# First attention with one pass of scores and transposed exponentials, and a new order at the second attention's start

## What is computed

```python
attn = jnp.einsum('bhqd,bhkd->bhqk', q, k) * SCALE      # first attention
mask = jnp.triu(jnp.full((s, s), -jnp.inf), k=1)
attn = softmax(attn + mask, axis=-1)
out = jnp.einsum('bhqk,bhkd->bhqd', attn, v)
...
logits = xf @ router_w.T                                 # experts
top_vals, top_idx = jax.lax.top_k(logits, 2)
out = out + combine[:, e:e + 1] * y                      # y: expert e's gated MLP
...
x = x + attn_a(layernorm(x)); x = x + ffn(layernorm(x))
x = x + attn_b(layernorm(x)); x = x + ffn(layernorm(x))
```

## Time and profile before

| | |
|---|---|
| median of three runs | 893.17 us (891.84 to 893.41) |
| the profiled execution | 890.42 us, its span 888.8 us |
| PE busy over the span | 778.6 us (88%) |
| DVE, ACT, POOL busy | 355.7, 285.2, 249.7 us |
| the chain that ended last | PE 80%, DVE 7%, DMA 5% |

### The profile page before, as it was taken

How to read it: one execution, slowest core, us unless ns; L and a number is a source line. 1 busy time by engine, 2 the same in 40 slices (tenths; PEclk the granted TensorE clock), 3 DMA queues, 4 the chain that set the end, 5 groups by cost and what they waited for, 6 DMA issues and landing times.

```text
span 888.8 us, 14689 instructions
## 1 busy us (share of the span) xinstructions
PE 778.6 (88%) x4924; PEld 592.6 (67%) x4925; DVE 355.7 (40%) x902; ACT 285.2 (32%) x527; POOL 249.7 (28%) x322
## 2 busy tenths in 40 slices
PE   5999999999989999999936389988879999999990
PEld 3777777787757677777725257666656767777760
DVE  4452553544434222222246477676463422212211
ACT  2103114031423334334222124534534234343321
POOL 1541043143034222212133313253641411211213
PEclk9999999999999999999977689999998999999995
DMA  7389933036971143002030722220401101110004
GB/s 191 68 259 329 318 100 92 10 78 234 340 199 49 40 164 117 34 25 77 18 107 18 216 50 52 51 65 7 163 29 39 66 31 35 35 35 24 30 19 148
DMA packets 48124, 88.10 MB, mean 99 GB/s; under 512 B 8913, under 2 KB 37329, under 8 KB 45937
## 3 DMA queue, kind: packets, MB, share of 16 engines
q1 hardware_dynamic: 36743, 54.56, 21.8%
q0 software_dynamic: 7568, 30.97, 9.5%
q10 hardware_dynamic: 3760, 1.87, 0.7%
HBM read 52.04 MB, written 35.03 MB: 98 GB/s over the span
## 4 chain that ended last, share of the span: by engine, by line
PE 80%; DVE 7%; DMA 5%; issue 2%; ACT 2%; POOL 2%; SPq 1%; ACTq 0%; POOLq 0%; DVEq 0%
PE bank L1423 24%; PE bank L1450 13%; PE bank L912 10%; PE bank L465 4%; PE bank L513 4%; PE bank L1436 4%; PE bank L525 2%; PE bank L455 2%; PE bank L546 2%; PE bank L511 2%; PE bank L589 2%; DVE XN L609 2%; PE bank L563 1%; DMA q_parts<-XN 1%; PE bank L1410 1%
## 5 line engine op out<-in xcount | busy, mean ns | idle before, releaser
L1423 PE MATMUL bank<-wgu,R 128*128 x736 | 224.8, 458 | 0.8 <-ACT R L1458 0.7
L1423 PEld LDWEIGHTS bank<-wgu,R 128*128 128x128 f32 x736 | 137.6, 192 | 66.0 <-issue 3.8
L1450 PE MATMUL bank<-R 112*128 (+1 forms) x552 | 127.0, 379 | 1.2 <-ACT R L1472 1.2
L1450 PEld LDWEIGHTS bank<-R 112*128 112x128 f32 (+1 forms) x552 | 104.4, 190 | 22.3 <-issue 1.7
L1488 DVE TENSOR_TENSOR R<-R,bank 128x344 f32<-128x344 f32 x92 | 47.2, 513 | 175.6 <-PE bank L1423 165.4
L658 ACT ACTIVATE PTR<-bank 128x512 f32<-128x512 f32 x144 | 78.8, 598 | 96.3 <-PE bank L513 83.2
L1399 POOL DMA_INDIRECT rows_out<-R,XN x46 | 45.4, 988 | 168.1 <-ACT R L1480 156.5
L1495 DVE COPY R<-bank 112x512 f32<-112x512 f32 x46 | 31.8, 690 | 103.8 <-PE bank L1436 103.8
L609 DVE TENSOR_REDUCE XN<-bank 128x2 f32<-128x512 f32 x96 | 63.2, 685 | 9.1 <-PE bank L465 9.1
L1466 ACT ACTIVATE R<-bank 128x344 f32<-128x344 f32 x92 | 41.9, 458 | 76.9 <-PE bank L1423 76.7
L829 POOL TENSOR_SCALAR_AFFINE_SELECT PTR<-PTR 128x512 f32<-128x512 f32 x64 | 39.7, 645 | 91.7 <-ACT PTR L658 91.6
(11 more groups left out here) (169 smaller groups left out, 1195.5 us busy)
## 6 DMA issues: line engine op xcount, KB each, us to landing
wgu<-in_wgu SPq DMA_DIRECT2D x10, 1376.0 KB, 15.5
slots_in<-wgu POOLq DMA_DIRECT2D x1, 9088.0 KB, 27.5
row_of_slot<-in_unused POOLq DMA_DIRECT2D x2, 4544.0 KB, 17.7
R<-slots_in SPq DMA_DIRECT2D x46, 128.0 KB, 2.0
wgu<-R SPq DMA_DIRECT2D x32, 128.0 KB, 2.4
R<-R SPq DMA_DIRECT2D x32, 128.0 KB, 2.4
R<-in_wd SPq DMA_DIRECT2D x8, 448.0 KB, 6.8
PTR<-rows_out SPq DMA_DIRECT2D x12, 256.0 KB, 4.5
```

Of the source, the lines that this page charges most:

```text
L1423: last = nc.tensor.matmul(BK[2 * half + gu][:, 0:IH], xsT[:, p, kk, :], wgu[:, bass.ds(e * (KD * GU) + (kk * GU + gu * I + half * IH), IH) ...
L1450: last = nc.tensor.matmul(down_bank(i)[:, 0:D], hT[0:CH[c], p, c, :], wd[0:CH[c], bass.ds(e * (6 * D) + c * D, D)], start=c == 0, stop=c == 5)
```

## The change

In the first attention the second pass, the split of the maxima and its transposes are gone. The scores of a group go to `bank0` to `bank2`; DVE takes the maxima and multiplies them by the scale (`maxima_a_vector`); ACT takes the exponentials with the maximum as a bias for each partition, in eight instructions for a group in place of three (`exps_a_scalar`), into a buffer in SBUF that exists once (`rows_of`: a part of expert 2's place, and `wob`). PE transposes the buffer in twelve pieces into `bank3` to `bank5` (`turned_tensor`), and ACT (two banks) and DVE (one) copy them to `PTR` (`moved_scalar`, `moved_vector`). One loop with n = 0 to 17 goes over the 16 groups of all batches: in step n PE does the scores of group n, the transposes of n-1, the turned output of n-3 and the value product of n-2. The finished batch b is projected at n = 4b + 7, normalised and routed at 4b + 8 and 4b + 9. Both projections for the first two batches stand ahead of the loop; the third's and fourth's are behind n = 3 and n = 7, and the next scores wait until they are evacuated. Expert 2 and `wob` are loaded later.

In the second attention the last part of q has a place of its own (`last_parts`, in `PTR`), so its split does not wait for an earlier store; DVE's wait for the stores moves from ahead of `parts_vector` to n = 1, and ACT gets one ahead of its first exponential; SP's order is shown below.

On PE, in the middle of the first batch, the second pass over one group of four heads stood like this before: one mask per bank, then for each head a product with the shift and the score product again (bank3 to bank5; the rows of bank4 and bank5 go on in the same way), and the value products into bank6.

The diff, cut to its core:

```diff
+        vaug3 = room(2 * KD * GU + 1024, 2 * HA * 32)
+        values_a = [vaug, vaug3, vaug2, vaug]
+
+        def rows_of(b):
+            o = 4 * HA * S // 2
+            two = room(2 * KD * GU, 1024) if b < B - 1 else R1[:, o:o + 1024]
+            return [two[:, 0:512], two[:, 512:1024], wob[:, :, :].rearrange("p k n -> p (k n)")]
...
-                elif i == 0 and g >= 2:
-                    nc.tensor.wait_ge(s["maxima"], b * 3 * G + 3 * (g - 1))
-                elif i == 0 and b > 0:
-                    nc.tensor.wait_ge(s["exps"], (b - 1) * 3 * G + 3 * (G - 1 + g))
+                else:
+                    later(nc.tensor, s["exps"], max(3 * (b * G + g - 1) + i + 1, 0))
...
-        def attend_a_tensor(b):
-            max_tensor(0, b)
-            nc.tensor.wait_ge(AT[0]["max_e"], b + 1)
-            for g in range(GA):
-                if g < 2 and b < B - 1:
-                    items = [i for i in BY_V if i < ITEMS - 3 or g == 1]
-                    nc.tensor.wait_ge(PA["evac_v"], (b + 1) * len(BY_V) + len(items))
...
+        RUN_A = B * GA
+
+        def turned_tensor(b, g):
+
+            s = AT[0]
+            n = b * GA + g
+            src = rows_of(b)
+            nc.tensor.wait_ge(s["exps"], 3 * n + 3)
+            if g == GA - 1 and b + 2 < B:
+                nc.tensor.wait_ge(PA["evac_v"], (b + 3) * len(BY_V))
+                nc.tensor.wait_ge(PA["evac_s"], (b + 3) * len(BY_S))
+            for i in range(2):
+                later(nc.tensor, s["moved_s"], max(2 * (n - 1) + i + 1, 0))
+                for j in range(2):
+                    c = 2 * i + j
+                    nc.tensor.transpose(BK[3 + i][:, j * S:j * S + P], src[0][:, c * P:(c + 1) * P], ident[:, :])
+                    last = nc.tensor.transpose(BK[3 + i][:, j * S + P:(j + 1) * S], src[1 + i][:, j * S:j * S + P], ident[:, :])
+                last.then_inc(s["turned"], 1)
+            later(nc.tensor, s["moved_v"], n)
+            for j in range(4):
+                o = (j % 2) * S + P
+                last = nc.tensor.transpose(BK[5][:, j * P:(j + 1) * P], src[1 + j // 2][:, o:o + P], ident[:, :])
+            last.then_inc(s["turned"], 1)
...
+        def attend_a_tensor():
+            for n in range(RUN_A + 2):
+                if n < RUN_A:
+                    scores_tensor(0, *of(n))
+                b = batch_at(n, 7)
+                if b is not None:
+                    project_tensor(0, b)
+                b = batch_at(n, 8)
+                if b is not None:
+                    norm_tensor(1, b)
+                ranked = batch_at(n, 9)
+                if ranked is not None and n < RUN_A:
+                    rank_tensor(1, ranked)
+                if 1 <= n <= RUN_A:
+                    turned_tensor(*of(n - 1))
+                if n >= 3:
+                    b = batch_at(n, 8)
+                    if b is not None:
+                        nc.tensor.wait_ge(LN[1]["evac"], b + 1)
+                    if ranked is not None and n < RUN_A:
+                        nc.tensor.wait_ge(FF[1]["slot"], ranked + 1)
+                    if ranked is not None and n >= RUN_A:
+                        nc.tensor.wait_ge(FF[1]["copied"], ranked + 1)
+                    out_t_tensor(0, *of(n - 3))
+                if n >= 2:
+                    pv_tensor(0, *of(n - 2))
+                b = batch_at(n, 6)
+                if b is not None:
+                    all_t_tensor(0, b)
+                b = batch_at(n, 8)
+                if b is not None:
+                    nc.tensor.wait_ge(AT[0]["divided"], n - 2)
+                    logits_tensor(1, b)
+                if ranked is not None and n >= RUN_A:
+                    nc.tensor.wait_ge(AT[0]["divided"], n - 2)
+                    rank_tensor(1, ranked)
+                if n < RUN_A and n % GA == GA - 1 and n // GA + 2 < B:
+                    project_a_tensor(n // GA + 2)
+            nc.tensor.wait_ge(FF[1]["slot"], B - 1)
...
+        def maxima_a_vector(b, g):
+            s = AT[0]
+            n = b * GA + g
+            bank = BK[0:3]
+            for i in range(3):
+                nc.vector.wait_ge(s["scores"], 3 * n + i + 1)
+                q, h, m = (0, 4 * g, 4) if i == 0 else (1, 4 * g + 2 * (i - 1), 2)
+                link(nc.vector.tensor_reduce(nrem[:, q, h:h + m], bank[i][:, :].rearrange("p (n s) -> p n s", n=m),
+                                             AX, ALU.max, negate=True))
+                nc.vector.tensor_scalar(nmax[:, q, h:h + m], nrem[:, q, h:h + m], SCALE_A, None,
+                                        ALU.mult).then_inc(s["maxima"], 1)
+
...
+        def moved_scalar(n):
+            s = AT[0]
+            for i in range(2):
+                nc.scalar.wait_ge(s["turned"], 3 * n + i + 1)
+                if i == 0:
+                    later(nc.scalar, s["pv"], max(n - 1, 0))
+                nc.scalar.activation(PT[:, n % 2, i, :], BK[3 + i][:, :], ACT.Copy).then_inc(s["moved_s"], 1)
...
+        def exps_a_scalar(b, g):
+            s = AT[0]
+            n = b * GA + g
+            dst = rows_of(b)
+            if g == 0 and b == B - 1:
+                nc.scalar.wait_ge(PA["placed_k"], B * PLACED_K)
+            for i in range(3):
+                nc.scalar.wait_ge(s["maxima"], 3 * n + i + 1)
+                if i == 0:
+                    later(nc.scalar, s["turned"], 3 * n)
+                q, h, m, w = (0, 4 * g, 4, P) if i == 0 else (1, 4 * g + 2 * (i - 1), 2, S)
+                for j in range(m):
+                    last = nc.scalar.activation(dst[i][:, j * w:(j + 1) * w], BK[i][:, j * w:(j + 1) * w], ACT.Exp,
+                                                bias=nmax[:, q, h + j:h + j + 1], scale=SCALE_A)
+                last.then_inc(s["exps"], 1)
...
+        def attend_a_vector():
+            for n in range(RUN_A + 2):
+                b = batch_at(n, 8)
+                if b is not None:
+                    normed_vector(1, b)
+                if n < RUN_A:
+                    maxima_a_vector(*of(n))
+                b = batch_at(n, 7)
+                if b is not None:
+                    add_vector(0, b)
+                    stats_vector(1, b, (AT[0]["added"], b + 1))
+                ranked = batch_at(n, 9)
+                if ranked is not None and n < RUN_A:
+                    slots_vector(1, ranked)
+                if 1 <= n <= RUN_A:
+                    moved_vector(n - 1)
+                if n >= 3:
+                    divide_vector(0, *of(n - 3))
+                if n >= 2:
+                    pv_vector(0, *of(n - 2))
+                b = batch_at(n, 8)
+                if b is not None:
+                    logits_vector(1, b)
+                    largest_vector(1, b)
+                if ranked is not None and n >= RUN_A:
+                    slots_vector(1, ranked)
+                if n < RUN_A and n % GA == GA - 1 and n // GA + 2 < B:
+                    project_a_vector(n // GA + 2)
+            full_tiles_vector(1)
...
+        def attend_a_scalar():
+            for n in range(RUN_A + 2):
+                b = batch_at(n, 8)
+                if b is not None:
+                    evac_scalar(1, b)
+                if n < RUN_A:
+                    exps_a_scalar(*of(n))
+                if 1 <= n <= RUN_A:
+                    moved_scalar(n - 1)
+                b = batch_at(n, 6)
+                if b is not None:
+                    out_scalar(0, b)
+                b = batch_at(n, 7)
+                if b is not None:
+                    root_scalar(1, b)
+                if n < RUN_A and n % GA == GA - 1 and n // GA + 2 < B:
+                    project_a_scalar(n // GA + 2)
...
-            nc.vector.wait_ge(PB["stored0"], 16 * 3)
-            nc.vector.wait_ge(PB["stored1"], 16 * (PARTS + 1))
             parts_vector(2, 0)
...
+                if n == 1:
+                    nc.vector.wait_ge(PB["stored0"], 16 * 3)
+                    nc.vector.wait_ge(PB["stored1"], 16 * (PARTS + 1))
                 if n >= 1:
                     pv_vector(2, (n - 1) // GB, (n - 1) % GB)
...
         def attend_b_scalar():
             max_scalar(2, 0)
+            nc.scalar.wait_ge(PB["stored0"], 16 * 3)
             for n in range(RUN):
...
             def store(i):
                 nc.scalar.wait_ge(s["lo"], i + 1)
+                if i == B:
+                    nc.scalar.wait_ge(s["stored0"], 16 * 2)
...
-                    elif i >= 2:
-                        nc.scalar.wait_ge(s["stored0"], 8 * i)
+                    elif i == 2:
+                        nc.scalar.wait_ge(s["stored0"], 16)
...
-            if b == 0:
-                nc.sync.wait_ge(PB["lo"], 2)
-                rows = k_r[0].rearrange("(j n i) h s -> n (i h) j s", j=2 * PARTS, n=PARTS)
-                for n in range(PARTS):
-                    nc.sync.dma_start(rows[n], qparts[0:32, 1, :, :]).then_inc(PB["stored1"], 16)
...
             if b == 0:
                 q_rows(0)
-                q_rows(1)
```

(15 more changed lines are left out.)

169 lines of the change are left out of this document (47 added, 122 removed).

## The result

The changed kernel takes 863.59 us (median of four runs, 859.38 to 872.76) against 892.5 for the kernel before, run beside it (890.19 to 893.41): a ratio of 0.9666, interval 0.9624 to 0.9707. With the six runs of the first experiment there are ten, from 859.0 to 872.8, with a median of 866.8; that is some 0.972 of the median before in the same two sets of runs (891.5). The kernel before, run beside every experiment, stayed between 888.7 and 897.0.

What follows compares the result with a forecast made beforehand. PE was taken to bound the first attention, DVE the second attention's start; 890.42 us less 17 (first expert tile earlier) and 7 (second attention) gave 866.4, and 2.75 up to the runs' median about 869; range 857 to 880.

Steps and rivals of the forecast that it cites:

- the likeliest case: Whole kernel: the median lies at 862 to 875 us, with 869 in it; chance 0.60.
- The step of the loop: First attention: one group's step takes 6.1 us, PE idling some 0.7; ends 5.9 and 6.8.
- The circle of one buffer: First attention: scores, transposes, overlap, four exponentials and hand-overs follow one another because the buffer exists once; 6.1 us.
- The twelve transposes: First attention, each step on PE: twelve transposes take 1.32 us, from four taking 0.44.
- the estimate of 901: First attention: at the skill's 275 ns, twelve transposes take 3.3 us, a step 8.1, the time some 32 more.
- I charge no clock for the loop: First attention's loop: PE's waits of 0.7 in 6.1 us leave the granted clock at 1.00; no cost.
- The rival of the falling clock: First attention's loop: at 1.2 GHz a step is 10.5 us, not 6.1; all sixteen give about 940; chance 0.05.
- The new wait for the root: First attention, n = 11: ACT's late square root delays PE's normalised rows by 2 us (0 to 4).
- The weights: Experts: weights are there by 213 us, needed at 238; a cover of 25 us, later loads cost nothing.
- The 7: Second attention's start: DVE's first maximum comes at about 501, not 507.75; worth 7 us (5 to 8).
- No wait bites: First attention: step 5.43 us, nothing lost to root or clock; gain 24 + 15, about 854; chance 0.12.
- DVE slowed by sharing PSUM: First attention's loop: DVE's work becomes 7.5 us a step, not 4.5; time about 891; chance 0.03.

Runs made afterwards that it cites:

- the first experiment: The changed kernel run once more with no edit, six runs: 868.25 us, ratio 0.9686.
- two_buffers: The changed kernel with a second buffer of exponentials for every other group, in expert 1's place, which is loaded last: 854.84 us, ratio 0.9591.
- tail_order: The changed kernel with the third batch's root, logits and rank put ahead at the end of the first attention: 860.1 us, ratio 0.9655.
- tail2_warm: tail_order with DVE's tile list right behind the slots and idle transposes ahead of first scores, third batch's normalising and first expert tile: 860.75 us, ratio 0.9657.
- gap0: The changed kernel with sixteen idle transposes in PE's wait ahead of the first scores: 863.93 us, ratio 0.9682.
- gap0_again: gap0 run once more, unchanged, for the count of runs: 860.08 us, ratio 0.966.
- the fill: The sixteen idle transposes ahead of the first scores, added to the changed kernel: 863.93 us in gap0, 860.08 us in gap0_again.
- second_part: The kernel before with only the second attention's edits: 883.63 us, ratio 0.9911.
- second_sp_old: second_part with SP's order as in the kernel before, both halves of q ahead of k's rows: 885.21 us, ratio 0.9934.

## Why the prediction was right, and where it was not

The time, 869 forecast, lies in the ten runs, and the likeliest case, 862 to 875, came in. The mechanism of the loop was right; that the number fits so well is in part luck, as the sum shows. Its steps:

- **The step of the loop.** Forecast 6.1 with 0.7 of waiting; measured 5.85 with 0.29 in a plain step. ACT's exponentials of 128 columns took 368 ns, 390 was taken. The circle of one buffer was the right mechanism: two_buffers breaks it.
- **The twelve transposes.** 1.32 forecast; from 206.94 to 208.26 twelve and the next product's start are 1.32 apart. The figure of 275 ns in the Trainium skill ("TensorE: Matmul & The Clock Gate", "Part 4: PE-mode transpose") agrees with how long one of this kernel's f32 transposes lasts, 0.27. But transposes overlap and start 0.11 apart, and the clock stands at 1.00 there. So the estimate of 901, which takes twelve such durations one behind the other, and the comparison by which the row "speaks for two fifths of that duration" mix a duration with the distance between starts.
- **"I charge no clock for the loop"** is the step that failed. The rival of the falling clock came in for two stretches, not for the loop: 9 us in the profiled execution. Its price was fair: the second step costs 4.0 more at the lower clock, and 4.4 was taken. The waits of 0.3 to 0.7 that I weighed are harmless (1.00 from 75 to 160); the first fall stands right behind the wait of 1.77 ahead of the first scores, which I had priced as time and not as an occasion. The second, from about 167, begins 9 us behind a wait of 1.38; what sets it off was not tried. The new wait for the root, priced at 2 as time, is an occasion too, in three other profiles.
- **The sum.** I had the last step ending at 210.4, so a start of 204.3 for group 15. Where the clock holds through the loop (tail_order, tail2_warm) it starts at 200.2 and 199.8, with one later fall (gap0, gap0_again) at 203.0 and 202.3, in the profile at 210.14. A projection was put at 20.5, is 20.6 by its own row and took 20.8. The new wait for the root was put at 2: the step with it is 9.39, the one a batch earlier 7.56, 1.8 less. The tail from the start of group 15 to the slots was put at 22.7 and is 22.0 to 23.1. The first tile was put at 238: 235.4 and 237.0 with the fill, 245.1 without.
- **The luck.** The changed kernel's profile gains 10.8 up to the first tile and 6.9 behind it, those with the fill 18.9 and 20.5, and 7.3 and 8.9; the forecast was 17 and 7. So the gain of 24 is 2 to 5 too small where the start holds the clock and 6 too large where the clock falls twice. 869 lies among the five runs above 868, in which the clock fell or was low, and comes from a sum in which it does not fall; the five other runs take 859 to 866.
- **The weights** were ready, as forecast, 24 ahead of the first tile (25 forecast).
- **The second attention.** The 7 is right (6.1 in the whole, 7.9 by the ratio of second_part). The reason was half right. What I described, the rows of k landing as before, is second_sp_old: scores at 500.29 and the first maximum at 501.35, where I had 500.46 and 501. In the change itself the scores come earlier (4.2 in second_part; counted from the first tile, 3.9 there and 2.2 in the whole), the end of DVE's split releases the first maximum, and each of the two edits alone is worth some 6.
- **The other rivals.** *No wait bites* had 854, and two_buffers measures 854.84, but from another base: it is 5 to 9 under the runs with the fill, where the rival took 15 off. No run shows DVE slowed by sharing PSUM: its maxima of 512 columns take 690 to 691 ns, 692 before.

## What to carry to other kernels

Where a buffer exists once, write the circle of its producers and readers as one sum and compare it with the busiest engine's work; then ask what the same buffer does at the loop's end, where nothing hides it. Price a wait of PE ahead of dense work not only as its length: look at the granted clock behind such waits, and run several times. When a wait for a transfer goes, ask whether the transfer was late by itself or by what was issued beside it, since reordering the queue may be worth as much as a new buffer.

## What the hardware showed unexpectedly

One and the same program spread from 859 to 873 us, and in each of the two sets the mean clock sorts the runs; in both profiles, at 872, the clock fell right behind a wait of 1.77 to 1.78 us. The kernel before, with a wait of 1.38 at the corresponding place, stayed within 8.3 us and held 1.00 from 57 to 245 in its profile. Idle transposes in the wait kept the clock in four profiles of four, and in tail2_warm 28 of them, with nothing else on PE, went with its rise from 0.50 (228 to 229) to 1.00 (230 to 231). In the tail a transpose costs 0.21 at the lower clock and 0.11 at the higher. A store of 384 KB held its reader for 11.8 us with a copy of 864 KB issued 1 us behind it and the second half's rows ahead of that, and at most 4.5 where both came later.
